# Another placement of a batch's pieces in the slots of two attention layers

## What is computed

```python
x = x + xattn0(layernorm(x), ctx, ctx)   # 16 heads of 16, low-rank terms added to Wq, Wk, Wv, Wo
x = x + ffn0(layernorm(x))               # sqrt((x@cos(theta))**2 + (x@sin(phi))**2)
x = x + xattn1(layernorm(x), ctx, ctx)   # 16 heads of 16, rotary positions on q and k
x = x + ffn1(layernorm(x))               # quantised weights and activations, gelu
# attention: softmax(q k^T / 4) v, then the output projection
```

## Time and profile before

| what | value |
|---|---|
| median of three runs | 1924.36 us |
| the profiled execution's own time | 1927.03 us |
| its span, first to last instruction | 1925.3 us |
| PE busy | 1665.8 us, 87% |
| VectorE busy | 1314.7 us, 68% |
| ScalarE busy | 1219.2 us, 63% |
| GpSimd busy | 844.9 us, 44% |
| exponentials of the two attention layers (L590) | 1024 instructions, 16 a batch |
| mean granted TensorE clock | 0.914 of full speed |

### The profile page before, as it was taken

The page is one execution under the profiler, slowest core; times in us unless marked ns, Lnnn a source line. Parts: engine busy times, 40 slices in busy tenths (PEclk is TensorE's granted clock), DMA queues, the critical chain, the costliest instruction groups (busy, mean ns, idle before and its releaser), DMA issues. The chain is left out here.

```text
span 1925.3 us, 38948 instructions
## 1 busy us (share of the span) xinstructions
PE 1665.8 (87%) x13992; PEld 1256.1 (65%) x13992; DVE 1314.7 (68%) x2567; ACT 1219.2 (63%) x2194; POOL 844.9 (44%) x670
## 2 busy tenths in 40 slices
PE   4899999999999879869999999999989838884987
PEld 3666666666666567646666666666666526663977
DVE  6676777777777658655676666766766546776986
ACT  1366666666666568636666666666666518885875
POOL 3344454545454130235556665666566112221432
PEclk8699999999999789968899899999998759997999
DMA  8466666676766320056666667666765214557775
GB/s 250 108 150 148 154 149 149 159 152 145 154 153 147 90 66 1 22 100 136 141 148 146 147 138 147 152 144 143 148 145 125 59 34 175 218 218 284 252 261 188
DMA packets 152485, 281.34 MB, mean 146 GB/s; under 512 B 39904, under 2 KB 66144, under 8 KB 144096
## 3 DMA queue, kind: packets, MB, share of 16 engines
q1 hardware_dynamic: 152304, 278.96, 57.5%
HBM read 89.99 MB, written 59.77 MB: 78 GB/s over the span
## 5 line engine op out<-in xcount | busy, mean ns | idle before, releaser
L690 DVE TENSOR_REDUCE L_negm<-L_s_bank 128x2 f32<-128x512 f32 x1024 | 665.9, 684 | 402.1 <-PE L_s_bank L480 393.8
L590 ACT ACTIVATE L_prob<-L_t_bank 128x512 f32<-128x512 f32 x1024 | 576.7, 601 | 276.6 <-PE L_t_bank L498 269.9
L480 PE MATMUL L_s_bank<-L_kst,L_qst 48*128 48x256 f32 x2048 | 466.0, 334 | 52.2 <-DVE L_negm L690 35.3
L498 PE MATMUL L_t_bank<-L_qst,L_kst 50*128 50x256 f32 x2048 | 456.9, 331 | 21.4 <-DMA L_qst<-L_mT 19.4
L480 PEld LDWEIGHTS L_s_bank<-L_kst,L_qst 48*128 48x128 f32 x2048 | 310.0, 198 | 205.9 <-DVE L_negm L690 93.3
L498 PEld LDWEIGHTS L_t_bank<-L_qst,L_kst 50*128 50x128 f32 x2048 | 305.4, 198 | 38.7 <-DMA L_qst<-L_mT 19.8
L566 PE MATMUL L_eo<-L_prob,L_vext 128*17 128x256 f32 x4096 | 264.1, 394 | 5.4 <-ACT L_prob L590 5.4
L362 POOL TENSOR_TENSOR L_kqr<-L_kqr,L_cs 128x1024 f32<-128x1024 f32 x32 | 75.7, 2366 | 303.0 <-DMA L_kqr<-L_kq 303.0
L566 PEld LDWEIGHTS L_eo<-L_prob,L_vext 128*17 128x17 f32 x4096 | 106.0, 99 | 104.5 <-issue 12.7
L600 ACT ACTIVATE L_osb<-L_eo 128x512 f32<-128x512 f32 x128 | 76.5, 598 | 150.5 <-PE L_eo L566 150.5
L1280 PE MATMUL G_acc<-G_w_out,G_hhl 128*128 128x256 f32 x1024 | 130.2, 285 | 46.4 <-DVE G_hhl L1249 46.2
(11 more groups left out here) (161 smaller groups left out, 2696.7 us busy)
## 6 DMA issues: line engine op xcount, KB each, us to landing
L_kst<-L_hl SPq DMA_DIRECT2D x384, 128.0 KB, 3.5
L_qst<-L_hl SPq DMA_DIRECT2D x384, 128.0 KB, 4.2
hidden_scratch<-G_hid SPq DMA_DIRECT2D x32, 1024.0 KB, 3.9
G_hid<-hidden_scratch SPq DMA_DIRECT2D x32, 1024.0 KB, 7.4
c_scratch<-L_cT SPq DMA_DIRECT2D x32, 512.0 KB, 2.9
L_rb<-r_scratch SPq DMA_DIRECT2D x64, 256.0 KB
L_cT<-c_scratch SPq DMA_DIRECT2D x32, 512.0 KB, 3.3
L_kqr<-L_kq SPq DMA_DIRECT2D x64, 256.0 KB, 4.5
```

The source lines that it names most:

```text
L480: mm = pe.matmul(s_bank[k % 2][:, t, :], qst[n % 2][rows, j, t, P * qt:P * (qt + 1)], kst[n % 2][rows, j, t, :], start=True, stop=True)
L498: mm = pe.matmul(t_bank[k % 2][:, t, :], kst[n % 2][rows, j, t, P * kt:P * (kt + 1)], qst[n % 2][rows, j, t, :], start=True, stop=True)
L590: act.activation(prob[h][:, kt, j, :, :], t_bank[k % 2][:, :, :], ACT.Exp, scale=HD ** -0.5).then_inc(sem["act_p"], 1)
L690: dve.tensor_reduce(negm[:, h, 0, :].rearrange("p (j t q) -> p j t q", j=HJ, t=KT)[:, j, :, qt], s_bank[k % 2][:, :, :], AX.X, ALU.max, ne ...
```

## The change

Only the three tables change: every piece of both layers may stand in another iteration or slot. No instruction is added or taken away; in layer 0 `bn` and `ag` go from three iterations behind to four, so the loop of layer 0 has one iteration more at its end, in which almost nothing is left to do. Two lines of the table and two of the banks:

```diff
-     "rb": (-1, 14), "ym": (-3, 0), "yh": (-3, 2), "yl": (-3, 4), "o0": (-2, 5), "o1": (-2, 7), "xa": (-2, 15),
+     "rb": (-2, 6), "ym": (-4, 0), "yh": (-4, 1), "yl": (-4, 7), "o0": (-3, 1), "o1": (-3, 7), "xa": (-3, 15),
...
-    {"xT": 0, "q": 2, "k": 1, "v": 2, "mT0": 2, "mT1": 2, "o": 1},
-    {"xT": 2, "q": 1, "k": 0, "v": 0, "mT0": 0, "mT1": 1, "o": 2},
+    {"xT": 0, "q": 0, "k": 0, "v": 2, "mT0": 2, "mT1": 2, "o": 1},
+    {"xT": 0, "q": 1, "k": 2, "v": 1, "mT0": 1, "mT1": 2, "o": 0},
```

## The result

The changed kernel takes 1898.99 us, the median of four runs (1897.28 to 1908.63), against 1924.23 for the kernel before on the same chip: 0.9875 of it, with a 95% interval of 0.9833 to 0.9917. The profiled execution has 1900.1 us and a span of 1898.3. The forecast was 1897 and 1900.0. The sum came out, by luck: two of its four terms lie outside the bounds given for them, the errors cancel, and the experiments show that the reason given for the largest term was too simple.

What follows compares the result with a forecast made beforehand. Bounds: PE in layer 0, waiting in a loop over GpSimd; in layer 1 a loop from `hl` over SP's DMAs to `hh`. 1927.0 - 29 - 5 + 5 + 2 = 1900.0, median 2.7 lower: 1897 us, range 1880 to 1930.

Steps and rivals of the forecast that it cites:

- Layer 0, -29 forecast: Layer 0's even iterations go from 18.7 to 17.7 us, times 28: 29 us less, from 14 to 39.
- The new wait of k: Layer 0: k on PE waits for GpSimd's `cl`, one buffer, 0.15 to 0.2 us an iteration.
- The wait for `yl`: Layer 0: PE's idle time before the output projection (L465), 0.80 us an iteration, goes.
- a gain of 0.3: Layer 0: `o` has its own bank and VectorE's pieces leave slots 5 to 7; bounds 0 and 0.3 us, 0.3 taken.
- half of the 0.25: Layer 0: half of PE's other idle time, 0.25 us an iteration, goes too, taking 17.85 to 17.7.
- the break between pair groups: Layer 0: PE's pair groups are broken up nine times instead of eight, about 0.1 to 0.2 us a break, 0.15 taken.
- Layer 1, -5 forecast: Layer 1: 0.2 of the 1.0 us above the loop's 20.4 goes, times 28: 5 us less, bounds 28 less and 30 more.
- the second: Layer 1: PE waits for `hh` every turn, lower clock covers q and k, turns of 22.5 us: 1931 us, chance 0.19.
- its mild form: Layer 1: the second rival in half of the turns only, 1914 us; half of its 0.19 chance.
- Start, +5 forecast: Start: VectorE's `xTl` now before the statistics, first maximum from 52.67 to about 59: 5 us more, bounds 0 and 8.
- made up: Start: part of the delay is regained, since the first iteration with maxima has k before it and q early.
- `pe1` step: Between layer 0 and feed-forward: last batch's `pe1` moves behind the angles' root, `rd` waits: 2 us more, bounds 0 and 4.

Runs made afterwards that it cites:

- o0_later: Kernel before, in layer 0 only the output projection's halves moved from slots 5 and 7 to 9 and 11: 1934.37 us, ratio 1.005.
- xn_behind: Kernel before, in layer 0 GpSimd normalises x behind `yl` instead of ahead of `ym`: 1933.22 us, ratio 1.0048.
- ym_ahead: Kernel before, in layer 0 `ym` and `yh` ahead of the context's split, `yl` behind, output projection an iteration later in its old slots: 1918.77 us, ratio 0.996.
- these five: Five layer 0 edits of the kernel before, the last two built on the third: 1934.37, 1933.22, 1918.77, 1933.66 and 1960.32 us.
- q1_spread: Changed kernel, in layer 1 `xTl` in slot 13, `ke` in slot 7, turned copy issued earlier, q's second half in slot 3: 1863.05 us, ratio 0.9669.
- four such steps: Cumulative edits to the changed kernel: `xTl` earlier, `ke` and turned copy earlier, q's second half earlier, SP and start order: 1889.66, 1869.2, 1863.05, 1827.86 us.
- stats_first: Changed kernel, VectorE's four statistics at the start taken one, two, one after the first three iterations, not none, two, two: 1899.63 us, ratio 0.9891.
- the last kernel: q1_spread with the start order of stats_first and, in layer 1, SP's `ctx` in slot 4 and `ml1` in slot 7: 1827.86 us, ratio 0.9504.

## Why the prediction was right, and where it was not

**Layer 0, -29 forecast, -23 measured in the first 28 iterations.** The new wait of k was sized right (0.15 to 0.2; 0.16). The wait for `yl` went. The sum of this term has slips of its own: costs of 0.2 and 0.15 against a gain of 0.3 make an iteration 0.05 longer and not shorter, so its own parts give 17.95, and 17.83 with half of the 0.25; that is 24 us. (1.0 times 28 is 28. The room before `o0` is 1.62 + 1.98 + 0.68 - 1.26 = 3.0 us and not 2.5, and PE reaches `o0` 1.31 us before `yl` ends; the 1.47 run to the start of `o0`.) 17.83 is what was measured, but not by these parts: the maxima are waited for by 0.27 more, the break between pair groups counted as a cost of 0.15 was not seen, and PE's busy time fell by 0.34. And "the 0.80 are gone" treats the wait before L465 as time that nothing else needs. o0_later, xn_behind and ym_ahead show that it was not free to take in the old placement: loops of nearly the same length lay behind it (`hl` to `qe`, `rb` to `ym`), and taking the first away alone gained 0.15 us an iteration at most. The forecast spoke of the room of `rb` and of `ym` in GpSimd's idle time and of no loop over `qe`. What the changed kernel has beyond these five is on PE above all k in v's old place, q in slots 3 and 5 and `o0` in slot 1; which of it the gain needs stays open. The size was near by the sum, the reason was a part of it.

**Layer 1, -5 forecast, -1.5 measured.** The choice of little rather than all or nothing was right, and so were the level of 21.0 to 21.5 and the clock (0.92 forecast, 0.94). Two things are in it that cancel: full turns became 1.1 us shorter (19.9 for 21.0), the others longer (22.5 for 21.9). The step that failed is one that is not in the text at all: `xTl` and `o0` in one bank and one slot, which the tables show. Their 1.2 us an iteration were missed. Of the rivals the second came in its mild form, without its cost to the total. PE's long wait in the pair groups moved from slot 0 to slot 6, as said: 9.7 us in ten waits for the exponentials, beside shorter ones for the maxima in slots 3 and 5.

**Start, +5 forecast with 8 as the bound, +9.5 measured.** The step is the one on VectorE's order. The first maximum was put at 59 and came at 61.20: the delay of 6.3 was right, and 2.2 came on top, since two copies of statistics took 1.76 and 0.86 us instead of 0.18 (below). And nothing of it was "made up" in the first iteration with maxima: from the first maximum to the first exponential it took 22.8 us against 21.9. The term was mis-sized by these two.

**Middle, +2 forecast, -12 measured.** The `pe1` step was looked at and the last iterations were not. Of the 11.9 us, 6.0 lie in the iteration before layer 0's last and 1.7 in the two ahead of it. Another 4.0 lie behind layer 0's last exponential, where PE waits 2.01 us for ScalarE at its first stop in the feed-forward part (L823) and waited 4.34 before; a cost of 2 us for `pe1` is not to be seen. In the iteration before the last PE has less to do, and in the kernel before `o0` waits 2.08 us for `yl` and the clock is at the lower level for much of it; the changed kernel keeps the full one. Rows and stretches of the kernel before (the first three) and of the changed one:

```profile
641.07 0.58 PE L498 MATMUL L_t_bank<-L_qst,L_kst 50*128 50x256 f32 x1
...
643.94 0.55 PE L465 MATMUL L_misc<-L_bohl,L_pick 128*128 128x256 f32 x1 [2.08 <-POOL L_yhl L412]
...
638.00:660.00 22.00, 17.79 (x146) 11.55 (x142) 12.93 (x26) 10.71 (x22) 5.96 (x6) 0.69 0.40 98
```

```profile
623.00:639.00 16.00, 13.36 (x147) 8.51 (x148) 12.77 (x26) 10.54 (x20) 3.18 (x3) 1.00 0.58 135
```

The wait is not what brings the lower clock there: it begins at 641.86, and the granted clock is 0.50 from 640.8 to 641.8 already, where a matmul of a pair group takes 0.58 us for the usual 0.28 to 0.38. Nor does taking the wait away keep the clock: in o0_later `o0` waits for nothing in this iteration, which takes 19.2 us at a clock of 0.82, and q1_spread, with the changed tables of layer 0, takes 18.0 us at 0.81 where the changed kernel takes 15.5. What decides it stays open. So the errors were +4.5, +6, -14 and +3.5 us, and it is luck that they cancel: the time was right to 2 us, and 12 of the 27 us between the two profiled executions come from a place that the forecast counted as a loss.

## What to carry over

A wait in front of an engine that is busy to 94% can be the longest of several loops, not a sum of money: before it is booked as a gain, write down the length of the next loop through the same engine, and what its work covers elsewhere. In a placement table look for two pieces that share a buffer and stand in the same slot; that can be a new wait, and here the bank table showed it. And where the clock falls with the waits as well, take them away in order, each read off the trace of the step before: layer 1 went from 21.3 to 19.15 us an iteration in four such steps, while layer 0 resisted five.

## What was not expected of the hardware

A copy of 28 numbers a row on VectorE took 1.76 us instead of 0.18, and ended at 42.02 with GpSimd's subtraction, which ended at 41.99 (start, duration; the third line is a copy of the kernel before, with GpSimd idle beside it):

```profile
39.62 2.37 POOL L409 TENSOR_TENSOR L_hl<-L_kq,L_hl 128x1024 fp32r<-128x1024 f32 x1
...
40.26 1.76 DVE L643 COPY stats<-L_mvt 128x28 f32<-128x28 f32 x1
...
46.52 0.18 DVE L643 COPY stats<-L_mvt 128x28 f32<-128x28 f32 x1
```

A second one took 0.86 from 47.91, to 48.77, and GpSimd's ran from 47.47 to 48.73. In stats_first one took 1.75 us, to 42.27, and GpSimd's ended at 42.24. The Trainium skill, "SBUF — State Buffer", section "SBUF: two separate sides", says that GpSimd and VectorE, in some of VectorE's instructions, share a pair of ports as an exclusive lock, for which the one that starts later waits through the other's whole instruction. These rows agree in that the copy ends behind GpSimd's instruction, by 0.03 to 0.04 us, which is less than the 0.18 that it takes alone.

The clock does not follow the length of a wait. In the changed kernel PE waits 1.26 us before `o0` in a stretch whose granted clock is 1.00 (1153 to 1158 us), and 0.59 in slot 6 ahead of the stretch at 0.50 shown above:

```profile
1153.00:1158.00 5.00, 3.74 (x36) 3.00 (x32) 4.96 (x11) 4.24 (x9) 2.38 (x2) 1.00 0.62 147
```

The Trainium skill, "TensorE: Matmul & The Clock Gate", section "HAM oscillation — how this bites in real kernels", tells of a kernel in which every wait for a DMA between two bursts of matmuls brings the lower clock. Those waits are longer than any that PE has in the even turns of the changed kernel, where the longest is 2.35 us, so no run here tries that case; yet 15 of these 27 turns lose the full clock. In the last kernel, with the same matmuls in another order, it is 3 of 27.
